# Softmax weights, masked scores and one layer's z kept in PSUM and changed in place, norms on GpSimd, and new instruction orders, in a two-layer graph kernel

## Chip, cores and metric

The kernel runs on one core of a Trainium2 chip. The metric is the time of one launch in microseconds on the device. All 128 graphs are handled by that core in one program.

The core's engines run their own instruction streams and meet through semaphores: TensorE (PE) multiplies into PSUM, eight banks of 512 float32 columns per partition; VectorE (DVE) and ScalarE (ACT) read and write PSUM and SBUF; GpSimd (POOL) works on SBUF; SyncE (SP) issues the DMAs of this kernel.

## What is computed

128 graphs of 128 nodes with 384 features. First a two-layer graph attention (L0), residual and norm, then a 12-head attention (L1), residual and norm:

```python
# L0, for l in 0, 1
u_left  = einsum('bih,bjh->bij', h, h @ W_left[l].T)  / sqrt(384)
u_right = einsum('bih,bjh->bij', h, h @ W_right[l].T) / sqrt(384)
u = u_left * triu(adj) + u_right * swap(triu(adj, 1))
e = exp(u) * adj
ctx = (e / (e.sum(2) + 1e-10)) @ (h @ W_lin[l].T + b_lin[l])
h = relu((ctx - mean) / (std(ddof=1) + 1e-3) * a + b)
x = layernorm(x + h)
# L1
p = softmax(q k^T / sqrt(384) + 2 * adj)   # a row of scores that are all 0 gives 0
x = layernorm(x + (p v) @ Wo.T + bo)
```

## The kernel before

**Tiling.** Graphs go in groups of four (`GROUP`), 32 groups. A pass of the program (`body`, once per engine) handles L0 of one group, L1 of the group before it, and the last pieces of L1 (the `TAIL`: pv, to, po, norm and store of graph 3) of the group before that. There are 34 passes: the first has no L1, the last two no L0. All float32 products are made of three f16 products (hi x hi, hi x lo, lo x hi), so nearly every PSUM result is read twice: ScalarE rounds it to the f16 `_hi` half, VectorE subtracts that from the PSUM value and writes the `_lo` half.

**Stages.** nl(l, 0..5): the left and right products of layer l, 9 matmuls of 512 columns each. hl(l, b): the linear product, 9 of 384. u(l): scores of L0. ctx(l, b): attention times h_lin, whose 385th column is the denominator; `den` takes its reciprocal, ScalarE scales the result (z), `bn` and `z_variance` give mean and variance. Layer 0's z is normed (`norm_z`), transposed on TensorE (th) and put through Relu; layer 1's z goes through `scale_z`, `shift_z`, `resid` (Relu and residual into x1), `y_bn`, `y_variance`, `resid_norm` and `x1_norm`, is split (`x1t`) and turned by two DMA transposes into xT. qk(0..5), v(b): the products of L1. scores(b): 36 small matmuls into the four banks `SC`, 12 heads of 128 columns; VectorE reads them with a custom instruction that adds the bias, negates, and keeps the row's extreme in `nmax`, into `s[b % 2]`. exps: ScalarE's exponents from s. pt: the f16 halves of the exponents. `turn_p`: two DMA transposes of them, pT. pv(b), to(b), po(b): weights times v, transpose, output product. `rs_of` makes 1/sum, set to 0 for an empty row, `live_of` the test for that; `folds` adds s up over the columns on GpSimd in three steps. `po` and `po_stats` on VectorE add the residual and take the last norm's statistics, `y2_power` (GpSimd) the root, `fin` the norm, `store` the DMA out.

**Order and waits.** There is no scheduler at run time: each engine's `body` is a list of calls written out by hand, and each engine runs its list in order. A PSUM bank is used by many stages in turn, in the order of the table `BANK_USES`; before its first matmul into a bank, TensorE waits for the signal in `READ` of the use before. Before the change a bank of scores was free at `s_ok`, VectorE's first read; exps wrote a single SBUF buffer `w`, pt wrote its halves over `s[b % 2]`, so that VectorE's scores(b + 2) waited for the transposes of graph b and for live(b):

```python
dve.wait_ge(live_ok.sem, of.upto(live_ok, n + 1))
dve.wait_ge(pT_in[b % 2].sem, of.upto(pT_in[b % 2], 32 * (n // 2 + 1)))
```

z and x1 were one SBUF buffer each for both layers and for two groups: ctx(0, b) waited for y_ok, and resid for y2_ok.

In the rows, L1322 is any product of `product`, L1332 a transpose, L1386 u, L1446 scores, L1463 pv, L596 ScalarE's copy whatever it copies, L883 and L881 VectorE's lo halves, L923 and L529 pt on VectorE and GpSimd, L948 rs, L1002 nmr of the last norm, L721 fin, L518 folds, L372 the transpose of pT_lo.

## Time and profile before

| | us |
|---|---|
| median of 3 runs | 2750.87 (2749.57 to 2752.33) |
| the profiled execution | 2750.55 |
| its span, first to last instruction | 2748.8 |
| PE, DVE, ACT, POOL busy in the span | 2581.7, 2356.8, 1863.5, 1655.0 |
| granted TensorE clock, mean | 0.986 |

The time of the profiled execution is 1.7 us more than its span. A row of the page or of the grouped view reads: line, engine, operation, output<-inputs, shape, count, busy time and mean ns of one, idle time of the engine before it and what ended most of that. The matmuls of a stream overlap, so the sum of their lengths is more than the time that they take.

### The profile page before, as it was taken

The page shows a single profiled execution, that of the slowest core. Times are in us where ns is not written, and L with a number is a line of the kernel's source. Part 1 is how long each engine was busy: PE and PEld are TensorE (multiplying, and loading weights), DVE is VectorE, ACT ScalarE, POOL GpSimd, SP SyncE. Part 2 cuts the span into 40 slices and gives each one's busy share as a digit, 9 for nine tenths or more (in the row PEclk, how much of TensorE's full clock was granted, in tenths as well). Part 3 has the DMA queues.
Part 4 walks back from the last instruction along what each step waited for, and adds up shares of the span by engine and source line. Part 5 has one row for each costly group of instructions (what it writes and reads, how often), then busy time and mean ns, then how long its engine had stood idle before and what let it go on. Part 6 is the DMA issues. An engine that isn't in the chain of part 4 may idle for free.

```text
span 2748.8 us, 70524 instructions
## 1 busy us (share of the span) xinstructions
PE 2581.7 (94%) x25152; PEld 1527.9 (56%) x25152; DVE 2356.8 (86%) x8074; ACT 1863.5 (68%) x4395; POOL 1655.0 (60%) x1686
## 2 busy tenths in 40 slices
PE   6999999999999999999999999999999999999976
PEld 3555555555555555555555555555555555555543
DVE  4788988889888889888889888889888898888885
ACT  4666776667776667776667776667766677766664
POOL 3556665565666565766565755566655656665644
PEclk9999999999999999999999999999999999999986
DMA  4235343344443343443343443343433433433333
GB/s 157 53 88 104 71 101 86 76 96 82 93 92 92 69 106 73 101 90 85 79 104 70 105 92 74 90 101 73 98 90 77 96 83 92 93 92 71 84 79 67
DMA packets 557742, 242.33 MB, mean 88 GB/s; under 512 B 506704, under 2 KB 539472, under 8 KB 557392
## 3 DMA queue, kind: packets, MB, share of 16 engines
q1 hardware_dynamic: 557392, 237.83, 38.7%
q8 instruction: 200, 3.28, 0.5%
q14 instruction: 150, 1.23, 0.2%
HBM read 86.77 MB, written 25.17 MB: 41 GB/s over the span
## 4 chain that ended last, share of the span: by engine, by line
DVE 41%; PE 38%; issue 10%; ACT 5%; POOL 3%; DMA 2%; SPq 1%; DVEq 0%; ACTq 0%; POOLq 0%
PE psum L1322 36%; DVE nT_lo L883 4%; DVE rs L948 3%; DVE s L912 3%; DVE z L1093 2%; DVE x L1121 2%; DVE y L979 2%; DVE s L923 2%; DVE z L1102 2%; DVE xTin L1157 2%; PE psum L1446 2%; DVE st L987 2%; DVE hl_raw L896 1%; DMA pT_lo<-s 1%; DVE yst L1048 1%
## 5 line engine op out<-in xcount | busy, mean ns | idle before, releaser
L657 ACT ACTIVATE w<-s,nmax 128x128 f32<-128x128 f32 x1536 | 477.6, 391 | 29.6 <-DVE nmax L912 29.4
L1322 PE MATMUL psum<-hT_hi,w_hi 128*128 128x512 f16 x1152 | 439.9, 382 | 34.2 <-DVE nT_lo L883 20.8
L1322 PE MATMUL psum<-hT_lo,w_hi 128*128 128x512 f16 x1152 | 438.3, 380 | 0.0
L1322 PE MATMUL psum<-hT_hi,w_lo 128*128 128x512 f16 x1152 | 437.8, 380 | 0.0
L596 ACT ACTIVATE nT_hi<-psum 128x512 f16<-128x512 f32 x384 | 220.7, 590 | 303.8 <-PE psum L1322 303.8
L912 DVE CUSTOM_DVE_ANT_0 s<-psum,adj 128x128 f32<-128x128 f32 x1536 | 345.6, 284 | 23.0 <-PE psum L1446 19.3
L446 POOL TENSOR_TENSOR hl_lo<-hl_raw,hl_hi 128x384 fp32r<-128x384 f32 x256 | 238.7, 938 | 192.5 <-ACT hl_hi L596 192.5
L518 POOL TENSOR_TENSOR fold<-s 128x768 f32<-128x768 f32 x128 | 243.2, 1900 | 152.6 <-DVE nmax L912 137.2
L883 DVE SCALAR_TENSOR_TENSOR nT_lo<-psum,nT_hi 128x512 f16<-128x512 f32 x384 | 251.8, 683 | 29.5 <-ACT nT_hi L596 29.1
L596 ACT ACTIVATE z<-psum,rden 128x384 f32<-128x384 f32 x256 | 134.2, 575 | 184.5 <-DVE rden L1034 184.5
L529 POOL TENSOR_TENSOR s<-w,s 128x512 f16<-128x512 f32 x128 | 164.1, 1282 | 145.3 <-ACT s L596 145.3
L1322 PE MATMUL psum<-w_hi,hT_hi 128*128 128x384 f16 x768 | 250.5, 326 | 0.0
L1322 PE MATMUL psum<-w_hi,hT_lo 128*128 128x384 f16 x768 | 250.3, 326 | 0.0
L1322 PE MATMUL psum<-w_lo,hT_hi 128*128 128x384 f16 x768 | 250.2, 326 | 0.0
L518 POOL TENSOR_TENSOR fold<-fold 128x384 f32<-128x384 f32 (+1 forms) x256 | 230.8, 901 | 20.1
L596 ACT ACTIVATE s<-w 128x512 f16<-128x512 f32 x384 | 228.8, 620 | 16.9 <-POOL fold L518 13.4
L1322 PE MATMUL psum<-xT_hi,w_hi 128*128 128x512 f16 x576 | 219.8, 382 | 13.2 <-DMA xT_lo<-xTin 13.2
L487 POOL TENSOR_TENSOR yrstd<-yvar,pw 128x4 f32<-128x4 f32 x32 | 32.4, 1013 | 329.8 <-DVE yvar L1068 329.8
L1322 PE MATMUL psum<-xT_lo,w_hi 128*128 128x512 f16 x576 | 219.1, 380 | 0.0
L1322 PE MATMUL psum<-xT_hi,w_lo 128*128 128x512 f16 x576 | 219.1, 380 | 0.0
L1322 PEld LDWEIGHTS psum<-hT_hi,w_hi 128*128 128x128 f16 x1152 | 112.6, 98 | 163.0 <-DVE nT_lo L883 24.4
L923 DVE TENSOR_TENSOR s<-w,s 128x512 f16<-128x512 f32 x256 | 176.7, 691 | 27.7 <-ACT s L596 27.1
(132 smaller groups left out, 7792.3 us busy)
## 6 DMA issues: line engine op xcount, KB each, us to landing
xTin<-xT SPq DMA_DIRECT2D x32, 768.0 KB, 4.4
xres<-x SPq DMA_DIRECT2D x32, 768.0 KB, 5.5
out<-y SPq DMA_DIRECT2D x128, 192.0 KB, 2.0
adjm<-adjM SPq DMA_DIRECT2D x32, 384.0 KB, 5.2
adjT_sb<-adjT SPq DMA_DIRECT2D x32, 256.0 KB, 4.7
adj<-adj SPq DMA_DIRECT2D x32, 256.0 KB, 3.3
x<-weights SPq DMA_DIRECT2D x4, 576.0 KB, 4.6
pT_hi<-s SPq DMA_TRANSPOSE x128, 3.8
```

Source lines behind the costliest of these rows:

```text
L446: nc.gpsimd.tensor_tensor(hl_lo[:, b, 0:FEAT], hl_raw[:, b], hl_hi[:, b, 0:FEAT].bitcast(f32), ALU.subtract).then_inc(hlr_lo[l].sem, 1)
L518: nc.gpsimd.tensor_tensor(fold[:, :, 0:n], src[:, :, 0:n], src[:, :, n:2 * n], ALU.add)\
L529: nc.gpsimd.tensor_tensor(p_lo[b % 2][:, part], w[:].rearrange("p h t -> p (h t)")[:, part], p_hi[b % 2][:, part], ALU.subtract).then_inc( ...
L596: return nc.scalar.activation(dst, src, ACT.Copy, scale=scale)
L657: last = nc.scalar.activation(w[:, m], s[b % 2][:, m], ACT.Exp, bias=nmax[b % 2][:, m:m + 1], scale=-1.0)
L883: nc.vector.scalar_tensor_tensor(dst, src, scale, rounded, ALU.mult, ALU.subtract)\
L912: last = nc.vector.tensor_tensor_reduce(out=s[b % 2][:, m], in0=psum[:, SC[j], c * TOK:(c + 1) * TOK], in1=adj2[:, b], scale=-1.0 / TEMPER ...
L923: nc.vector.tensor_tensor(p_lo[b % 2][:, part], w[:].rearrange("p h t -> p (h t)")[:, part], p_hi[b % 2][:, part], ALU.subtract).then_inc( ...
L948: nc.vector.scalar_tensor_tensor(rs[b % 2][:], live[b % 2][:], 0.0, rs[b % 2][:], ALU.is_gt, ALU.mult) .then_inc(rs_ok.sem, 1)
L979: nc.vector.scalar_tensor_tensor(y2[:, b % 2], bank("po", b)[:, 0:FEAT], 1.0 / WSCALE, x1[:, b], ALU.mult, ALU.add).then_inc(y2_ok.sem, 1)
L987: nc.vector.bn_stats(st2[:], y2[:, b % 2]).then_inc(y2st_ok.sem, 1)
L1322: last = mm(dst, a, b, start=(i == 0), stop=(i == total - 1))
```

## The change

- **Softmax weights in PSUM.** exps write the exponents back into the score bank they came from. pt is now per bank: ScalarE copies 384 columns to the f16 half in a buffer of its own, `p16[b % 2][:, 0]`, and VectorE subtracts it from PSUM into `p16[b % 2][:, 1]` (16 each per pass, none on GpSimd). A score bank is free at `pt_lo`.
- **u in PSUM**: masked and added in place (in two instructions and an addition for two graphs), exp_u reads PSUM. **Relu of th** is written back in place for th's lo half. **Layer 1's z** stays in its ctx bank until the residual has read it; that bank is free at `y_ok`.
- **x1 in two buffers** `xb`: x is loaded by DMA into the one that becomes x1 (`load_res`), the separate `xres` is gone.
- **live_of** only sums; the test for an empty row is two comparisons inside `rs_of`, with intermediates in unused columns of the pv bank; nmax and total get a buffer per graph.
- **Norms as (x - mean) * rstd**: nmr, ynmr and nmr2 are gone. fin and x1_norm move from ScalarE to GpSimd, the additions of 1e-5 from VectorE to GpSimd; the factor of the unbiased deviation moves into inv_std.
- **New orders** on all five engines and a new `BANK_USES`. On TensorE to(3) and po(3) of the tail move from among nl(0, .) to behind u(0), qk(0) ahead of ctx(0, .), hl(1, 0..1) ahead of scores(1), scores(3) behind nl(1, 5), hl(1, 3) stays behind to(1), po(1) and po(2) move among and behind ctx(1, .). On SP load_tri moves behind turn_p(0), store(3) ahead of turn_p(1).

```diff
-        READ = {... "u0": u_read[0], "u1": u_read[1],
-                "c0": z_ok[0], "c1": z_ok[1], "th": th_hi, "qk": qkr_lo, "v": v_sum, "s": s_ok,
+        READ = {... "u0": e_raw[0], "u1": e_raw[1],
+                "c0": z_ok[0], "c1": y_ok, "th": th_lo, "qk": qkr_lo, "v": v_sum, "s": pt_lo,
...
-            uses(("hl0", 0), ("qk", 2), ("s", 0, 4, 8, 12), ("to", 0, 2), ("po", 2)),
+            uses(("nl0", 5), ("u0", 0), ("qk", 2), ("s", 0, 4, 8, 12), ("to", 2), ("c1", 3)),
...
# ScalarE
                 for c in range(KB):
                     m = KB * j + c
-                    last = nc.scalar.activation(w[:, m], s[b % 2][:, m], ACT.Exp, bias=nmax[b % 2][:, m:m + 1],
+                    last = nc.scalar.activation(psum[:, SC[j], c * TOK:(c + 1) * TOK], s[b % 2][:, m], ACT.Exp, bias=nmax[b][:, m:m + 1],
                                                 scale=-1.0)
-            def pt(p, b, r):
-                act.wait_ge(fold1.sem, p.upto(fold1, b + 1))
-                act.wait_ge(p_ok.sem, p.upto(p_ok, TILES * b + r + 2))
-                copy(p_hi[b % 2][:, part], w[:].rearrange("p h t -> p (h t)")[:, part]).then_inc(pt_hi.sem, 1)
+            def pt(p, b, j):
+                act.wait_ge(p_ok.sem, p.upto(p_ok, TILES * b + j + 1))
+                copy(p16[b % 2][:, 0, KB * TOK * j:KB * TOK * (j + 1)], psum[:, SC[j], 0:KB * TOK]).then_inc(pt_hi.sem, 1)
# VectorE
                 if j == 0 and of.l1:
-                    dve.wait_ge(live_ok.sem, of.upto(live_ok, n + 1))
-                    dve.wait_ge(pT_in[b % 2].sem, of.upto(pT_in[b % 2], 32 * (n // 2 + 1)))
+                    dve.wait_ge(fold1.sem, of.upto(fold1, n + 1))
+                if of.l1:
+                    dve.wait_ge(p_ok.sem, of.upto(p_ok, n * TILES + j + 1))
...
+                nc.vector.tensor_tensor(p16[b % 2][:, 1, part], psum[:, SC[j], 0:KB * TOK], p16[b % 2][:, 0, part],
+                                        ALU.subtract).then_inc(pt_lo.sem, 1)
...
-                nc.vector.scalar_tensor_tensor(rs[b % 2][:], live[b % 2][:], 0.0, rs[b % 2][:], ALU.is_gt, ALU.mult)
+                nc.vector.scalar_tensor_tensor(rs[b % 2][:], total[b][:], 0.0, rcp, ALU.is_gt, ALU.mult)\
+                    .then_inc(live_ok.sem, 1)
+                nc.vector.scalar_tensor_tensor(peak, nmax[b][:], 0.0, rcp, ALU.is_lt, ALU.mult)\
+                    .then_inc(live_ok.sem, 1)
+                dve.wait_ge(live_ok.sem, p.upto(live_ok, 2 * b + 2))
+                nc.vector.tensor_tensor(rs[b % 2][:], peak, rs[b % 2][:], ALU.max).then_inc(rs_ok.sem, 1)
...
-                nc.vector.tensor_tensor(uLR[h][:], bank(f"u{l}", h)[:, 0:2 * TRI].rearrange("p (b c) -> p b c", b=2),
-                                        mask[:, 2 * h:2 * h + 2], ALU.mult).then_inc(u_read[l].sem, 1)
+                nc.vector.tensor_tensor(u_right[h][:], dst[:, :, TOK:TRI], mask[:, 2 * h:2 * h + 2, TOK:TRI], ALU.mult)\
+                    .then_inc(u_right_ok[l].sem, 1)
+                nc.vector.tensor_tensor(dst[:, :, 0:TOK], dst[:, :, 0:TOK], mask[:, 2 * h:2 * h + 2, 0:TOK], ALU.mult)\
+                    .then_inc(u_read[l].sem, 1)
...
+                nc.vector.scalar_tensor_tensor(z1(b), z1(b), mv[1][:, b, 0:1], lnrow[:, 0],
+                                               ALU.subtract, ALU.mult).then_inc(za_ok.sem, 1)
...
-                nc.vector.scalar_tensor_tensor(x1[:, b], z[:, b], 0.0, xres[:, b], ALU.max, ALU.add)\
+                nc.vector.scalar_tensor_tensor(xb[1 - p.odd][:, b], z1(b), 0.0, xb[1 - p.odd][:, b], ALU.max, ALU.add)\
# GpSimd
+            def fin(run, b):
+                pool.wait_ge(y2pow_ok.sem, p.upto(y2pow_ok, b + 1))
+                nc.gpsimd.tensor_scalar(y2[:, b % 2], y2[:, b % 2], mv2[:, b % 2, 0:1], rstd2[:, b % 2:b % 2 + 1],
+                                        ALU.subtract, ALU.mult).then_inc(fin_ok.sem, 1)
```

The orders at three places. First VectorE at the seam of two passes, behind the last statistics of ctx(1, .): L1056 / L1039 are the aggregates, L1093 / L1072 scale_z, L1102 / L1081 shift_z, L1121 / L1100 resid, L883 / L873 nl(0, .), L945 and L948 rs_of(3), L960 pv(3). Before:

```order
L1056 BN_AGGR mv1<-st1 128x2 [waits st_ok1] x4
L1058 TENSOR_SCALAR var1<-mv1 128x4 [waits mv_ok1]
L1093 SCALAR_TENSOR_TENSOR z<-z,mv1,lnrow 128x384 x3
L883 SCALAR_TENSOR_TENSOR nT_lo<-psum,nT_hi 128x4x128 [waits nl0_hi] x2
L945 RECIPROCAL rs1<-psum 128x12 [waits pv_full]
L948 SCALAR_TENSOR_TENSOR rs1<-live1,rs1 128x12 [waits live_ok,rcp_ok]
L1075 TENSOR_SCALAR sd_eps1<-sd1 128x4 [waits pow_ok1]
L1077 RECIPROCAL rstd1<-sd_eps1 128x4 [waits eps_ok1]
L960 TENSOR_TENSOR o1<-psum,rs1 128x4x3x32 [waits rs_ok,to_full]
L1093 SCALAR_TENSOR_TENSOR z<-z,mv1,lnrow 128x384
L1102 SCALAR_TENSOR_TENSOR z<-z,rstd1,lnrow 128x384 [waits za_ok,rstd_ok1]
L1102 SCALAR_TENSOR_TENSOR z<-z,rstd1,lnrow 128x384 [waits za_ok]
```

and after the change:

```order
L1039 BN_AGGR mv1<-st1 128x2 [waits st_ok1] x4
L1072 SCALAR_TENSOR_TENSOR psum<-psum,mv1,lnrow 128x384 [waits mv_ok1] x3
L1053 TENSOR_SCALAR sd_eps1<-sd1 128x4 [waits pow_ok1]
L1055 RECIPROCAL rstd1<-sd_eps1 128x4 [waits eps_ok1]
L1072 SCALAR_TENSOR_TENSOR psum<-psum,mv1,lnrow 128x384 [waits mv_ok1]
L1081 SCALAR_TENSOR_TENSOR psum<-psum,rstd1,lnrow 128x384 [waits za_ok,rstd_ok1]
L1081 SCALAR_TENSOR_TENSOR psum<-psum,rstd1,lnrow 128x384 [waits za_ok]
L1100 SCALAR_TENSOR_TENSOR xb0<-psum,xb0 128x384 [waits zb_ok,xres_in]
L1081 SCALAR_TENSOR_TENSOR psum<-psum,rstd1,lnrow 128x384 [waits za_ok]
L873 SCALAR_TENSOR_TENSOR nT_lo<-psum,nT_hi 128x4x128 [waits nl0_hi]
```

The z chain now comes ahead of nl(0, .), and rs_of(3) and pv(3), which wait for TensorE's pv(3), stand behind all of it.

Second VectorE from scores(0, 3) of graph 0 to the first tile of the next graph. After the change (L1089 is th, L1117 v, L913 pt, L924 the sum of live_of, L903 scores):

```order
L1089 TENSOR_TENSOR hT1_lo<-psum,hT1_hi 128x512 [waits th_raw,th_hi]
L1117 SCALAR_TENSOR_TENSOR v_raw<-psum,bias 128x384 [waits v_full,pv_full] x2
L913 TENSOR_TENSOR p16_0<-psum,p16_0 128x384 [waits pt_hi] x4
L1117 SCALAR_TENSOR_TENSOR v_raw<-psum,bias 128x384 [waits v_full,pv_full]
L924 TENSOR_REDUCE total0<-fold 128x12 [waits fold3]
L903 ISA s1,nmax1<-psum,adj2 128x128 [waits s_full,p_ok,fold1]
```

Before, the three v and th were followed at once by the next graph's scores, and graph 0's two pt stood behind three of its four tiles.

Third GpSimd from the last fold of a pass to the last v, where L473 / L475 is weigh, L483 / L485 e_rest, L446 / L448 hl(1, 3), L487 / L489 the powers. Before:

```order
L518 TENSOR_TENSOR fold<-fold 128x12x16 [waits fold2]
L473 TENSOR_TENSOR e<-e,adjT_sb 128x256 [waits e_raw1]
L487 TENSOR_TENSOR rstd<-var,pw 128x1 [waits y2var_ok]
L483 TENSOR_TENSOR e_lo<-e,e_hi 128x256 [waits e_ok1,e_hi_ok1]
L473 TENSOR_TENSOR e<-e,adjT_sb 128x256 [waits e_raw1]
L446 TENSOR_TENSOR hl_lo<-hl_raw,hl_hi 128x384 [waits hl1_hi]
L483 TENSOR_TENSOR e_lo<-e,e_hi 128x256 [waits e_ok1,e_hi_ok1]
L446 TENSOR_TENSOR hl_lo<-hl_raw,hl_hi 128x384 [waits hl1_hi]
L529 TENSOR_TENSOR s<-w,s 128x512 [waits pt_hi,p_ok]
```

and after:

```order
L522 TENSOR_TENSOR fold<-fold 128x12x16 [waits fold2]
L475 TENSOR_TENSOR e<-e,adjT_sb 128x256 [waits e_raw1] x2
L485 TENSOR_TENSOR e_lo<-e,e_hi 128x256 [waits e_ok1,e_hi_ok1] x2
L532 TENSOR_SCALAR var2<-mv2 128x1 [waits y2mv_ok]
L489 TENSOR_TENSOR rstd2<-var2,pw 128x1 [waits y2var_ok]
L541 TENSOR_SCALAR y2<-y2,mv2,rstd2 128x384 [waits y2pow_ok]
L448 TENSOR_TENSOR hl_lo<-hl_raw,hl_hi 128x384 [waits hl1_hi]
```

The subtraction of pt is gone from GpSimd's list, and fin(0) (L541) now stands between the last e_rest and hl_lo(3); three of the four hl_lo moved ahead of the last folds, and so did two biases and the lo halves of x.

## Rows read from the trace of the kernel before

**Rows 1.** The page: span, and busy us (share of the span) xinstructions

```profile
span 2748.8 us, 70524 instructions
...
PE 2581.7 (94%) x25152; PEld 1527.9 (56%) x25152; DVE 2356.8 (86%) x8074; ACT 1863.5 (68%) x4395; POOL 1655.0 (60%) x1686
```

**Rows 2.** The chain that ended last, in order of time: start, us, what

```profile
269.76 13.56 PE psum L1322 x63
...
2599.21 13.56 PE psum L1322 x63
```

**Rows 3.** Windows: stretch, us, busy (x) of each engine, PEclk, DMA share, GB/s

```profile
1185.50:1268.50 83.00, 80.00 (x787) 47.57 (x786) 72.96 (x252) 57.73 (x138) 51.62 (x53) 1.00 0.42 86
```

**Rows 4.** Timeline of TensorE: start, us, operation, [idle before <-releaser]

```profile
1221.72 0.23 PE L1446 MATMUL psum<-qk_hi 32*128 32x128 f16 x4
...
1233.71 0.55 PE L1332 MATMUL psum<-ident,o 128*128 128x128 f32 x3 [0.60 <-DVE o L960]
...
1239.54 0.41 PE L1322 MATMUL psum<-hl_hi,e_hi 128*128 128x386 f32 x1 [0.59 <-DVE y L979]
...
1242.87 0.39 PE L1322 MATMUL psum<-hT_hi,w_hi 128*128 128x512 f16 x1
...
1248.54 0.39 PE L1322 MATMUL psum<-hT_hi,w_hi 128*128 128x512 f16 x1 [0.71 <-DVE nT_lo L883]
```

**Rows 5.** The same timeline, first and last of 36 matmuls of qk

```profile
1191.13 0.39 PE L1322 MATMUL psum<-xT_hi,w_hi 128*128 128x512 f16 x1
...
1198.69 0.38 PE L1322 MATMUL psum<-xT_hi,w_lo 128*128 128x512 f16 x1
```

**Rows 6.** Small instructions: grouped by form; one line's min/median/max ns; the timeline

```profile
L948 DVE SCALAR_TENSOR_TENSOR rs<-live,rs 128x12 f32<-128x12 f32 x128 | 97.2, 760 | 4.6 <-DVE rs L945 0.2
...
L1002 DVE SCALAR_TENSOR_TENSOR nmr<-mv,rstd 128x1 f32<-128x1 f32 x128 | 55.3, 432 | 105.8 <-POOL rstd L487 105.8
...
L945 DVE RECIPROCAL rs<-psum 128x12 f32<-128x12 f32 x128 | 28.6, 223 | 1.0 <-PE psum L1463 0.7
...
L948 DVE SCALAR_TENSOR_TENSOR rs<-live,rs x128: 170/172/1810, 140.1 to 2737.4; 128x12 f32<-128x12 f32 x128
...
1221.58 1.81 DVE L948 SCALAR_TENSOR_TENSOR rs<-live,rs 128x12 f32<-128x12 f32 x1
...
1221.55 1.81 POOL L518 TENSOR_TENSOR fold<-s 128x768 f32<-128x768 f32 x1
```

**Rows 7.** VectorE's groups by form: busy us, mean ns

```profile
L883 DVE SCALAR_TENSOR_TENSOR nT_lo<-psum,nT_hi 128x512 f16<-128x512 f32 x384 | 251.8, 683 | 29.5 <-ACT nT_hi L596 29.1
...
L923 DVE TENSOR_TENSOR s<-w,s 128x512 f16<-128x512 f32 x256 | 176.7, 691 | 27.7 <-ACT s L596 27.1
...
L881 DVE TENSOR_TENSOR oT_lo<-psum,oT_hi 128x384 f16<-128x384 f32 x128 | 71.2, 556 | 11.1 <-ACT oT_hi L596 10.9
```

**Rows 8.** GpSimd's groups by form

```profile
L446 POOL TENSOR_TENSOR hl_lo<-hl_raw,hl_hi 128x384 fp32r<-128x384 f32 x256 | 238.7, 938 | 192.5 <-ACT hl_hi L596 192.5
...
L529 POOL TENSOR_TENSOR s<-w,s 128x512 f16<-128x512 f32 x128 | 164.1, 1282 | 145.3 <-ACT s L596 145.3
...
L502 POOL TENSOR_SCALAR adj<-adj 128x512 f32<-128x512 f32 x32 | 19.8, 619 | 12.8 <-DMA adj<-adj 10.2
```

**Rows 9.** ScalarE's groups by form

```profile
L657 ACT ACTIVATE w<-s,nmax 128x128 f32<-128x128 f32 x1536 | 477.6, 391 | 29.6 <-DVE nmax L912 29.4
...
L596 ACT ACTIVATE s<-w 128x512 f16<-128x512 f32 x384 | 228.8, 620 | 16.9 <-POOL fold L518 13.4
...
L721 ACT ACTIVATE y<-y,nmr,rstd 128x384 f32<-128x384 f32 x128 | 90.1, 704 | 51.6 <-DVE nmr L1002 50.8
...
L596 ACT ACTIVATE oT_hi<-psum 128x384 f16<-128x384 f32 x128 | 62.0, 485 | 42.2 <-PE psum L1332 41.3
```

**Rows 10.** Timeline of SP's DMA queue, the second transpose of graph 3

```profile
1242.74 1.42 SPq L372 DMA_TRANSPOSE pT_lo<-s  x1
```

**Rows 11.** The chain that ended last, in its last 70 us

```profile
2711.78 5.36 DMA pT_lo<-s
```

588 lines of the change are left out of this document (274 added, 314 removed).

## The prediction

> **What bounds the kernel now.** I read the page first: TensorE is busy 94% of the span, VectorE 86%, ScalarE 68%, GpSimd 60% [rows 1]. Then the chain that ended last: its long runs of matmuls come back at the same place of each pass, 28 passes in 2599.21 - 269.76 us, so a pass takes **83.2 us** [rows 2]; there are 30 such passes (pass 2 to pass 31), some 2,496 of the 2,749 us. Then the windows: in one pass TensorE is busy 80.0 of 83.0 us, VectorE 73.0, ScalarE 57.7, GpSimd 51.6 [rows 3]. The busy figure flatters TensorE: 36 matmuls of 512 columns start 0.216 us apart (7.56 / 35), but each is drawn 0.38 us long [rows 5], so after each wait some 0.165 us are counted that a stream would have overlapped. With about 14 waits a pass the work is 80.0 - 2.3 = **77.7 us**, and 5.5 us of a pass are waits. The change does not touch the matmuls, so 5.5 is all it can give, and only by making TensorE's inputs and banks ready sooner.
>
> Where the 5.5 us are: the timeline marks waits for o, y2 and nT_lo, all VectorE's work, in the last third and at the start of a pass [rows 4]; from scores(3) at 1221.7 to nl(0,0) at 1242.9, behind ctx(1,3), it takes 21.2 us [rows 4], of which about 18.4 are matmuls by their spacings, and from there to the matmul behind ctx(0,3) (1191.1 [rows 5], one pass of 83.0 on) it takes 31.3 for 29.3 of work. So some 4.8 us of the 5.5 lie in these two stretches.
>
> **The change part by part (us per pass).**
>
> *VectorE's small instructions.* rs<-live,rs has a median of 172 ns and a mean of 760; nmr, smaller still, a mean of 432. The timeline shows why: one rs took 1.81 us just while GpSimd ran a fold of 1.81 us [rows 6]. The excess over 0.17 is 0.59 x 4 = 2.4 and 0.26 x 4 = 1.0. nmr2 goes for good. That the new instructions of rs_of, which all have a PSUM operand, are not held is my choice: the row nearest to them, the reciprocal from PSUM in the same rs_of, has a mean of 223 ns [rows 6]. So I take all 3.4 as gone; the bound on the other side keeps the 2.4. Also gone: 13 instructions of about 0.15 (variance adds, nmr, ynmr, live), -2.0; new: two more in rs_of per graph, +1.0.
>
> The Trainium skill (SBUF — State Buffer, section "SBUF: two separate sides") says that a VectorE instruction with two SBUF inputs and a GpSimd instruction that reads SBUF exclude each other for a whole instruction, whichever starts first; only its first half is seen here, in the 1.81 beside 1.81. By that rule, GpSimd's stretched instructions shrink as well, since after the change only the four x1_lo subtractions have two SBUF inputs; if instead any small instruction could be held, the 2.4 would stay.
>
> *pt.* Before: 8 subtractions of 512 columns on VectorE (0.69 drawn, 0.61 apart) and 4 on GpSimd (1.28) [rows 8]. After: 16 of 384 columns on VectorE, priced as oT_lo, 0.556 drawn, 0.47 apart [rows 7]: 7.5 against 4.9, **+2.6** on VectorE, -5.1 on GpSimd. ScalarE: 16 copies like oT_hi (0.485) for 12 of 0.620: even [rows 9].
>
> *Operands in PSUM.* Scale, shift, residual, statistics, th and pt now read PSUM and some write it. A 512-column subtraction costs 0.683 with a PSUM input and 0.691 from SBUF [rows 7]: I take reads at no cost, bound +0.07 each. No row shows a VectorE or ScalarE write to PSUM; nearest, ScalarE's exp 0.391 [rows 9]: I take 0, bounds -0.06 to +0.06 per instruction. u is split in two, +0.8 in all.
>
> VectorE's sum: -3.4 - 2.0 + 1.0 + 2.6 + 0.8 = **-1.0**, from 73.0 to about 72.
>
> *Norms to GpSimd.* Six ScalarE instructions of 0.70 go (-4.2) [rows 9]; on GpSimd a tensor_scalar of 512 columns took 0.619, a two-input one of 384 took 0.938 [rows 8]. For 384 columns with one tensor input I take 0.47 (0.619 x 384/512), bound 0.94. Six of them and five small adds of 0.15: +3.6 (bound +6.4), against -5.1 for pt. GpSimd stays near 50.
>
> *What no longer waits.* scores(b+2) no longer waits on VectorE for the transposes of graph b or its live; exps no longer wait for the single w. In return a score bank is free only after exponent, copy and subtraction, not after the first read. So **scores(b+1) on TensorE now waits for pt(b,3)**, and everything behind it queues on TensorE.
>
> **Walking one pass in the new order.** I count from the end of ctx(1,3), with spacings: VectorE 0.47 for 384 columns, 0.60 for 512, 0.53 for scale and shift, 0.63 for three score tiles; exp 0.29; matmul products 1.94 (512), 1.46 (384), pv 0.9, scores 0.6, u 3.05, ctx 0.53.
>
> A, to the end of ctx(0,3), 28.8 of matmuls. VectorE: den, po and bn of the last graphs end at 4.4 (the four aggregates in), scale x3, inv_std, scale, shift x2, residual(0) at 8.8; then residual(1) 10.8 and residual(3) 12.3. z lies in the banks of nl(0,3), nl(0,4), nl(0,5), hl(0,1), and TensorE wants the first at 1.5 + 3.9 + 0.9 + 1.9 = 8.2, then 10.7 and 12.7: 0.6 us lost. x1_lo is done at 19.5; its transpose lands some 4 to 5.4 later (5.36 is one of the longest, [rows 11]), by 25, when qk(0) comes. u ends at 22, e_lo of the first pair is there at 26.5, ctx(0,0) starts at 27.4. I take 1.0 lost in all (before: 2.0).
>
> B, to scores(1), 19.1 of matmuls. th(0) finds z normalised at 35.7 and is due at 37. qk_lo(5) is ready at 41.0, 0.4 after TensorE wants it. Scores 0 on VectorE with th, v and the four pt end at 48.6; TensorE, with v(0..2) and hl(1,0..1) between, comes at 48.6. Lost: 0.5, no margin.
>
> C, to scores(3), 17.1. pt(1,3) ends at 56.8, scores(2) is due at 57.2; pt(2,3) 64.8 against 65.9. v_lo(0) from GpSimd 58.7 against 59.3. Lost: 0.3 to 0.4.
>
> D, to the end of ctx(1,3), 12.7. Here GpSimd is last: from s_ok(0) at 44.4 it runs four folds of 3.6, xt x3, four biases, v x3, hl x3 without a gap and reaches the end of fold(3) at 73.3, then two weigh and two e_rest of 0.7: e_lo(0) 75.5, e_lo(1) 76.2, rstd2 and fin(0), hl_lo(3) 78.3. TensorE is ready for ctx(1,0) at 75.5 and for ctx(1,3) at 78.6; hl(1,3) waits 0.3 for the bank that exp of u holds. Lost: 0.6 (before: 2.9). pt(3) is copied at 77.2, and the two transposes, 1.4 us of queue time each [rows 10] and about 4 from the second one's issue to its landing, are there 1.2 us before pv(3) is due.
>
> Sum: 77.7 + 1.0 + 0.5 + 0.4 + 0.6 = **80.2**; such a walk misses small gaps, so I say **80.3**, 2.9 less than now. 30 x 2.9 = 87.
>
> *Ends.* The first pass has no attention beside it; all products of hl(1,0) now need the whole of th_lo, and hl(0,3), hl(1,3) are the only cover for e: +1.5. In the last 150 us VectorE's z chain no longer stands behind pv(3) (-3) and VectorE's scores no longer wait for a transpose (5.36 us) [rows 11], but each scores waits for pt: -1. Together -2.5 (bounds -8 and +5).
>
> The profiled execution took 2750.6 us (span 2748.8), the median is 2750.9. 2750.6 - 87 - 2.5 = **2661**.
>
> **The rivals.**
>
> *GpSimd sets the end of the pass.* In D it has no slack: if its norm costs 0.94 instead of 0.47 (two of them before hl_lo(3): +0.9) and a fold 0.1 more than the spacing I used (+0.4), ctx(1,3) ends 1.3 to 1.6 later: 81.8, **2706**. For: the 36 us without a gap, and means of folds above their best. Against: GpSimd idles from there to the next pass's s_ok(0) often.
>
> *The score banks.* If exponent, copy and subtraction in a bank take 0.5 us longer than I priced, scores wait four times: 82.2, **2718**. For: no margin in B, and no row for writes to PSUM. Against: ScalarE has 54 of 80 us of work, and its copies with PSUM inputs are cheap.
>
> *Reads from PSUM cost more.* Priced from the bound, 0.07 on the 39 VectorE instructions whose input moves to PSUM is 2.7 us, of which 16 lie in A and some 10 in B and D without cover: +1.8, 82.1, **2715**. The rows speak against (0.683 and 0.691). The Trainium skill (VectorE: DVE Perf Modes, section "The TRN2 errata — SBUF-src ops pay a fixed extra latency per instruction") has 58 cycles fixed from SBUF and 120 from PSUM, which would do just this; the row disagrees and I follow the row.
>
> *Nothing is gained.* The held instructions were covered, and the new order only moves the waits: 83.1, **2747**. Against: the two stretches with 4.9 us of waits both wait for VectorE.
>
> *Slower.* SP's queue holds store(0) ahead of the transposes of graph 3, and store(0) now waits for GpSimd's fin(0), which stands behind fold(3), weigh and e_rest. If GpSimd is late, pT of graph 3 is late, pv(3) near the head of the next pass waits, and all of TensorE behind it. From 1.2 us of lateness it costs one for one, and from 1.2 + 2.9 = 4.1 us the kernel is slower than before. If fold(3) and fin(0) come 5.5 us later than walked: 84.6, **2791**. Against: before, the same queue held store(0), and pT_lo of graph 3, issued at 1242.74 [rows 10], was in time for pv(3), which stands two products of 1.94 behind 1242.87 [rows 4].
>
> **How the numbers follow.** Forecast (79.4 to 81.2 us a pass, 2632 to 2690): 0.62. GpSimd: 0.17. Score banks: 0.06. PSUM reads: 0.04. Nothing gained: 0.05. Slower: 0.06. Range: forecast, GpSimd and most of the two next, **2630 to 2718**. Faster by over 0.2% (5.5 us, about what a measurement of this kernel can tell): 0.89; same 0.05; slower 0.06.
>
> **What would show it.** A pass of 80.3 in the chain's repeats; rs and peak at about 0.17 without a long one; VectorE near 72 and ScalarE near 54 of a pass; exp not above 0.39; GpSimd's tensor_scalar near 0.47; TensorE's waits for o and y2 gone and the largest one at nl(0,3) for the residual. Wrong if TensorE waits for e_lo or hl_lo at ctx(1,.), for pt at scores, or for pT_lo at pv(3).

## The result, and the profile after

The changed kernel took **2730.44 us** (median; 2728.74 to 2731.18), the one before 2750.87. The ratio is 0.992, with a 95% interval of 0.990 to 0.995. So it is faster, by 20 us, where 90 were forecast: 2661 with a range of 2630 to 2718. The direction was right, the size was not, and the time lies outside the range.

The page after; its first lines answer to [rows 1]:

```profile
span 2728.7 us, 69288 instructions
...
PE 2572.6 (94%) x25152; PEld 1521.4 (56%) x25152; DVE 2275.4 (83%) x8170; ACT 1731.8 (63%) x4331; POOL 1792.6 (66%) x1910
...
POOL 41%; PE 32%; ACT 10%; issue 7%; DVE 6%; DMA 3%; SPq 1%; POOLq 0%; ACTq 0%; DVEq 0%
```

VectorE and ScalarE lost 81 and 132 us of busy time. GpSimd gained 138, though it gave up four large subtractions of each pass, and the chain that ended last now runs for 41% of the span through GpSimd, more than through any other engine; before, 3% of it did.

The length of a pass is read from the load of x^T, which SP issues once in each; two of them, 25 passes apart:

```profile
269.46 0.34 SPq L324 DMA_DIRECT2D xTin<-xT  x1
...
2330.63 0.34 SPq L324 DMA_DIRECT2D xTin<-xT  x1
```

(2330.63 - 269.46) / 25 = **82.45 us**; over the 24 passes without the first it is 82.42, and in the kernel before it was 83.19. So a pass gave 0.77 us where 2.9 were forecast: 30 x 0.77 = 23, and what lies outside the 30 passes grew by 3.0 (2748.8 - 30 x 83.19 = 253.1; 2728.7 - 30 x 82.42 = 256.1).

A window of one pass, the same columns as [rows 3]:

```profile
1258.00:1340.30 82.30, 79.41 (x785) 47.10 (x784) 70.31 (x255) 53.23 (x135) 55.35 (x60) 1.00 0.44 88
```

VectorE 70.3 (before 73.0), ScalarE 53.2 (57.7), GpSimd 55.4 (51.6) us. The groups by form (busy us, mean ns of one, idle before) show where the last number comes from:

```profile
L541 POOL TENSOR_SCALAR y<-y,mv,rstd 128x384 f32<-128x384 f32 x128 | 212.3, 1659 | 13.1
L550 POOL TENSOR_SCALAR xb<-xb,ymv,yrstd 128x384 f32<-128x384 f32 x64 | 112.7, 1766 | 3.5
L506 POOL TENSOR_SCALAR adj<-adj 128x512 f32<-128x512 f32 x32 | 19.9, 623 | 11.2 <-DMA adj<-adj 8.4
...
L522 POOL TENSOR_TENSOR fold<-s 128x768 f32<-128x768 f32 x128 | 232.4, 1815 | 364.0 <-DVE nmax L903 364.0
...
L936 DVE SCALAR_TENSOR_TENSOR rs<-total,psum 128x12 f32<-128x12 f32 x128 | 21.3, 167 | 4.4
L938 DVE SCALAR_TENSOR_TENSOR psum<-nmax,psum 128x12 f32<-128x12 f32 x128 | 21.6, 169 | 0.0
```

The norms (L541, L550) take **1.66 and 1.77 us each**, where the prediction had 0.47 with a bound of 0.94, from the row of adj, which is unchanged at 0.62 for 512 columns. The place in the pass does not make a fin long: the shortest of the 128 took 1.647 us, the longest 1.666. The small instructions of rs_of, 0.76 us before [rows 6], are down to 0.17, as forecast.

What the norms do to TensorE is seen at two places of each pass. First GpSimd and TensorE at the end of the pass (timeline: start, us, operation, [idle before <-releaser]):

```profile
1309.43 1.44 POOL L485 TENSOR_TENSOR e_lo<-e,e_hi 128x256 fp32r<-128x256 f32 x2
1310.84 0.23 POOL L532 TENSOR_SCALAR var<-mv 128x1 f32<-128x1 f32 x1
1311.15 0.58 POOL L489 TENSOR_TENSOR rstd<-var,pw 128x1 f32<-128x1 f32 x1
1311.84 1.67 POOL L541 TENSOR_SCALAR y<-y,mv,rstd 128x384 f32<-128x384 f32 x1
1313.47 0.87 POOL L448 TENSOR_TENSOR hl_lo<-hl_raw,hl_hi 128x384 fp32r<-128x384 f32 x1
```
```profile
1314.39 0.45 PE L1297 MATMUL psum<-hl_hi,e_hi 128*128 128x386 f32 x1 [0.82 <-POOL hl_lo L448]
```

fin(0) stands in front of hl_lo(3), and ctx(1,3) waits 0.82 us for that. Then, 25 us sooner, fin(3) in front of fold(1), whose sum VectorE awaits (total(1), 0.90 idle) with pt(1,3) queued behind it; pt(1,3) frees the score bank:

```profile
1285.51 1.66 POOL L541 TENSOR_SCALAR y<-y,mv,rstd 128x384 f32<-128x384 f32 x1
1287.13 1.81 POOL L522 TENSOR_TENSOR fold<-s 128x768 f32<-128x768 f32 x1
1289.03 1.67 POOL L522 TENSOR_TENSOR fold<-fold 128x384 f32<-128x384 f32 x2
...
1290.73 0.35 DVE L924 TENSOR_REDUCE total<-fold 128x12 f32<-128x192 f32 x1 [0.90 <-POOL fold L522]
1291.00 0.55 DVE L913 TENSOR_TENSOR p<-psum,p 128x384 f16<-128x384 f32 x1
...
1291.60 0.23 PE L1421 MATMUL psum<-qk_hi 32*128 32x128 f16 x4 [0.82 <-DVE p L913]
```

The wait names VectorE's p here; what set it is the fold on GpSimd that total(1), in front of that pt, had to wait for. Over the whole run (TensorE's waits: us in total, times, longest):

```profile
PE psum L1421 <- DVE p L913: 34.8, 32, 7.4
PE psum L1297 <- POOL hl_lo L448: 24.7, 31, 0.8
...
PE psum L1297 <- DVE xb L1100: 15.2, 30, 1.2
```

### The profile page after: what moved, and what is told of

It reads as the page before. It is cut to its first block, busy times and chain, and to the rows that moved or that the text cites. A ratio compares the mean times of both kernels' runs of the same rounds, so it can differ in the third digit from the quotient of the medians.

```text
span 2728.7 us, 69288 instructions
## 1 busy us (share of the span) xinstructions
PE 2572.6 (94%) x25152; PEld 1521.4 (56%) x25152; DVE 2275.4 (83%) x8170; ACT 1731.8 (63%) x4331; POOL 1792.6 (66%) x1910
## 4 chain that ended last, share of the span: by engine, by line
POOL 41%; PE 32%; ACT 10%; issue 7%; DVE 6%; DMA 3%; SPq 1%; POOLq 0%; ACTq 0%; DVEq 0%
PE psum L1297 28%; POOL fold L522 12%; POOL hl_lo L448 4%; POOL xb L465 4%; POOL y L541 4%; ACT psum L667 4%; POOL hT_lo L440 4%; POOL v_lo L456 3%; POOL rstd L489 3%; DMA xT_lo<-xTin 2%; PE psum L1361 2%; POOL mask L432 2%; POOL xb L550 2%; ACT p L612 2%; ACT hT_hi L712 2%
## 5 line engine op out<-in xcount | busy, mean ns | idle before, releaser
L667 ACT ACTIVATE psum<-s,nmax 128x128 f32<-128x128 f32 x1536 | 469.7, 363 | 75.8 <-DVE nmax L903 75.8
L522 POOL TENSOR_TENSOR fold<-s 128x768 f32<-128x768 f32 x128 | 232.4, 1815 | 364.0 <-DVE nmax L903 364.0
L1297 PE MATMUL psum<-hT_hi,w_hi 128*128 128x512 f16 x1152 | 438.2, 380 | 27.4 <-DVE xb L1100 15.2
L903 DVE CUSTOM_DVE_ANT_0 s<-psum,adj 128x128 f32<-128x128 f32 x1536 | 338.8, 286 | 28.7 <-PE psum L1421 28.5
L448 POOL TENSOR_TENSOR hl_lo<-hl_raw,hl_hi 128x384 fp32r<-128x384 f32 x256 | 237.0, 937 | 129.9 <-ACT hl_hi L612 129.7
L913 DVE TENSOR_TENSOR p<-psum,p 128x384 f16<-128x384 f32 x512 | 261.6, 547 | 23.9 <-ACT p L612 23.2
L873 DVE SCALAR_TENSOR_TENSOR nT_lo<-psum,nT_hi 128x512 f16<-128x512 f32 x384 | 247.9, 678 | 21.4 <-ACT nT_hi L612 21.4
L612 ACT ACTIVATE p<-psum 128x384 f16<-128x384 f32 x512 | 222.6, 481 | 1.8
L541 POOL TENSOR_SCALAR y<-y,mv,rstd 128x384 f32<-128x384 f32 x128 | 212.3, 1659 | 13.1
L522 POOL TENSOR_TENSOR fold<-fold 128x384 f32<-128x384 f32 (+1 forms) x256 | 204.0, 797 | 20.1
L612 ACT ACTIVATE qk_hi<-psum 128x512 f16<-128x512 f32 x192 | 114.7, 597 | 157.1 <-PE psum L1297 153.2
L1361 PE MATMUL psum<-nT_hi,hT_hi 128*64 128x192 f16 x1536 | 191.7, 248 | 1.4 <-DVE nT_lo L873 1.4
```

Of the source, the lines that this page charges most:

```text
L448: nc.gpsimd.tensor_tensor(hl_lo[:, b, 0:FEAT], hl_raw[:, b], hl_hi[:, b, 0:FEAT].bitcast(f32), ALU.subtract).then_inc(hlr_lo[l].sem, 1)
L522: nc.gpsimd.tensor_tensor(fold[:, :, 0:n], src[:, :, 0:n], src[:, :, n:2 * n], ALU.add)\
L541: nc.gpsimd.tensor_scalar(y2[:, b % 2], y2[:, b % 2], mv2[:, b % 2, 0:1], rstd2[:, b % 2:b % 2 + 1], ALU.subtract, ALU.mult).then_inc(fin_ ...
L612: return nc.scalar.activation(dst, src, ACT.Copy, scale=scale)
L667: last = nc.scalar.activation(psum[:, SC[j], c * TOK:(c + 1) * TOK], s[b % 2][:, m], ACT.Exp, bias=nmax[b][:, m:m + 1], scale=-1.0)
L873: nc.vector.scalar_tensor_tensor(dst, src, scale, rounded, ALU.mult, ALU.subtract)\
```

## The experiments

Times are medians; the kernel before took 2750.0 to 2752.1 beside them, and the difference to 2730.4 is taken straight, so differences of a few us between kernels say little. Ratios are against the kernel before of the same set of runs. The edits are shown shortened: buffer numbers and waits are left out. The three price lists ran once each, the others four or five times.

Three explanations were set against each other: (A) the length of GpSimd's norms, (B) score banks that come free too late whatever GpSimd does, (C) many small gaps that the walk had missed.

**fin_act.** `fin` on ScalarE, its bias formed on GpSimd.

```
-   nc.gpsimd.tensor_scalar(y2[b], y2[b], mean, rstd2, ALU.subtract, ALU.mult)
+   nc.gpsimd.tensor_scalar(nmr2, mean, rstd2, -1.0, ALU.mult, ALU.mult)
+   nc.scalar.activation(y2[b], y2[b], ACT.Identity, bias=nmr2, scale=rstd2)
```

> The last norm fin goes back to ScalarE (Identity with scale and bias); GpSimd instead forms its bias, one column, behind each power. All else as in the changed kernel. Theory A (GpSimd's norms of 1.66 us make the pass long: fin(3) in front of fold(1), fin(0) in front of hl_lo(3), fin(1) in front of z_power): TensorE's waits of 0.8 us at scores(2), 0.8 at ctx(1,3) and part of the 0.5 at nl(0,3) go, 1.3 to 1.8 us of a pass, 2675 to 2692 us against 2730. Theory B (the score bank is free too late because exponent, copy and subtraction stand on it, whatever GpSimd does): the wait for p at scores(2) stays above 0.6, the pass loses at most 0.5, 2715 or more. Theory C (the walk missed many small gaps): GpSimd gets shorter by 6 us of a pass and the time hardly moves, 2725 or more.

2727.9 (ratio 0.991, 0.990 to 0.993). The waits at scores(2) and ctx(1,3) shrank as A said (hl_lo: 24.7 to 0.2 us in all; p: 34.8 to 11.4), which rules B out as the cause of them. The time by itself does not: it lies in the ranges of B and C and not in that of A. Nearly all was given back, since TensorE now waited for pT_lo, 68.8 us in 59 pieces where the changed kernel waits 7.6:

```profile
PE psum L1443 <- DMA pT_lo<-p: 68.8, 59, 5.1
...
PE psum L1426 <- DVE p L918: 11.4, 3, 7.4
```

**x1n_act** and **norms_act.** The two norms of x1 on ScalarE, alone and with fin_act.

> Only the two norms of x1 go back to ScalarE, ahead of x1's four copies; GpSimd forms their bias columns. fin stays on GpSimd. Theory A: the copies of x1 end some 0.5 us sooner, the wait for xT_lo at qk(0) (0.4 us) goes, nothing else: 0.2 to 0.4 us of a pass, 2718 to 2725. Theories B and C: no change, 2728 to 2732. If ScalarE's two norms of 0.7 delay x1's copies instead: 2730 to 2740.

2724.1 (0.990, 0.989 to 0.992), as A said; the gain on 2730.4 is only 6 us.

> Both edits together: no norm is left on GpSimd. Theory A: the parts add up, 1.6 to 2.1 us of a pass, 2667 to 2682, near the 2661 that was forecast with norms of 0.47. Theory B: 2712 or more. Theory C: 2722 or more.

2717.5 (0.988, 0.986 to 0.989): far from A's number, and by its time alone in B's range (2712 or more). But the wait for p is at 11.4 us here too, as in fin_act, and what TensorE waits for is pT_lo, 66.8 us in 57 pieces. The trace shows SP's queue and the product that waits:

```profile
1312.48 0.35 SPq L307 DMA_DIRECT2D out<-y  x1
1312.93 1.31 SPq L373 DMA_TRANSPOSE pT_hi<-p  x1
1314.29 1.95 SPq L375 DMA_TRANSPOSE pT_lo<-p  x1
```
```profile
1318.63 0.18 PE L1452 MATMUL psum<-v_hi,pT_hi 128*128 128x33 f16 x1 [0.70 <-DMA pT_lo<-p]
```

pt_hi of graph 3 was written at 1310.5, but its transpose stands behind store(0), which waits for fin(0), done at 1312.46. That is the place of the prediction's slower rival.

**norms_act2.** store(0) behind the transposes of graph 3, y2_power(3) ahead of folds(0), fin(3) behind qk(4).

```
     turn_p(p, 2)
-    store(p, 0)
     turn_p(p, 3)
+    store(p, 0)
     store(p, 1)
```

> The kernel norms_act (2717.5 us, where TensorE waits 0.7 us at pv(3) and 0.3 at pv(2) for pT_lo) with three moves: store(0) behind the transposes of graph 3 in SP's queue, y2_power(3) ahead of folds(0) on GpSimd, fin(3) behind qk(4) on ScalarE, so that store(3) no longer holds the transposes of graph 1. If the gain of the norms' move was given back in SP's queue (theory A with the named rival of the prediction in place of it): both waits for pT_lo go, 1.0 us of a pass, about 2687; pass 80.4. If they only uncover the next wait (o, oT_lo or p): at least 2705.

**2780.1** (1.011, 1.010 to 1.013), slower than before. The move was mine and it broke something else: y2 has two buffers, po(2) on VectorE writes the one that store(0) reads, and all of VectorE queues behind it:

```profile
1337.96 0.56 DVE L986 SCALAR_TENSOR_TENSOR y<-psum,xb 128x384 f32<-128x384 f32 x1 [2.51 <-DMA out<-y]
```

TensorE then waits 2.42 us for the residual, and its granted clock falls behind that wait: 0.80, 0.50 and 0.84 in the 6 us from 1344, so for some us to the lower of its two levels, 1.2 GHz. Of 25 passes in the middle 16 have such a stretch; they took 84.3 us on average and the other nine 83.8, against 80.2 in norms_act3 below, so the clock is the small part of the loss. pool_order has it in 22 of 25 passes.

**norms_act3.** The same with three buffers of y2 (graphs 0 to 3 use 0, 1, 2, 1).

> norms_act2 (2780 us, where VectorE waits 2.51 us at po(2) for store(0), which the move behind the transposes of graph 3 made late) with three buffers of y2 for two, so that po(2) need not wait for store(0). All norms on ScalarE. If store(0)'s place is what gave the gain back in norms_act, and the shared y2 what lost it in norms_act2: the wait of VectorE for out<-y goes, no pT_lo wait at pv(3) or pv(2), 2670 to 2690 us. If neither: 2715 or more.

**2660.1** (0.967, 0.965 to 0.968), 10 us below the range that I gave. With no norm on GpSimd and the queue out of the way, the kernel runs where the forecast was. C falls with this: small gaps are not what kept the changed kernel 69 us from the forecast.

**pool_order**, **pool_order3** and **order_clean.** The norms stay on GpSimd at 1.66 us, at better places: y2_power(3) and fin(3) ahead of folds(0), fin(0) behind hl_lo(3), store(0) behind the transposes. pool_order has two y2 buffers and the mask behind z_power(1), pool_order3 three buffers, order_clean three buffers and the mask where it was.

> The changed kernel with its norms left on GpSimd at 1.66 us, and only its places changed: y2_power(3) and fin(3) ahead of folds(0), where GpSimd idles for 11 us; fin(0) behind hl_lo(3); the mask behind z_power(1), where GpSimd idles for 8 us; store(0) behind the transposes of graph 3. If it is the place of the norm that costs (what stands behind it): waits at scores(2), ctx(1,3) and part of nl(0,3) go, 1.3 to 1.8 us of a pass, 2677 to 2692 us. If it is GpSimd's load as such or VectorE's instructions stretched beside it: 2715 or more.

2816.4 (1.024, 1.023 to 1.026): the same wait for store(0) as in norms_act2 spoiled it.

> pool_order (2816 us: norms of 1.66 at better places on GpSimd, where VectorE waited at po(2) for store(0)) with three buffers of y2. If place decides (the norms cost by what stands behind them): 2665 to 2690. If their length decides wherever they stand: 2715 or more.

2721.4 (0.989, 0.988 to 0.991), and not clean either: the moved mask held a four-column VectorE instruction on the path to the residual.

```profile
1317.14 1.81 POOL L433 TENSOR_TENSOR mask<-adjm,keep 128x768 f32<-128x768 f32 x1
...
1317.21 1.76 DVE L1053 TENSOR_SCALAR sd_eps<-sd 128x4 f32<-128x4 f32 x1 [0.57 <-POOL sd L490]
```

> The changed kernel with subtract and multiply norms of 1.66 us on GpSimd, three y2 buffers, store(0) behind the transposes of graph 3, y2_power(3) and fin(3) ahead of folds(0), fin(0) behind hl_lo(3); the mask stays where it was. pool_order3 (2721) less the 1.6 us a pass that the mask cost there. If place decides: 2665 to 2685, as good as short norms. If length decides: 2715 or more. In between: both.

2702.9 (0.983, 0.981 to 0.984), in between: place alone (with the third buffer and the moved store) brings 27 of the 75 us by which the fastest kernel below beats the changed one, the rest needs shorter norms. The wait for hl_lo at ctx(1,3) is gone, but the one for the residual (xb) at nl(0,3) rose from 15.2 to 46.2 us in all: two norms now stand in front of z_power(1).

**The price lists** fin_forms, fin_forms2, fin_forms3: the changed kernel with its fins, and in the last two x1's norms, at the same places in other forms, most of which leave out a part of the norm.

> A price list, with wrong values: fin(0) on GpSimd as tensor_scalar with two constants, fin(1) with one per-partition column and one constant, fin(2) with one column alone, fin(3) as a tensor_tensor with the mean's column spread over 384 columns; the norms of x1 keep two columns. If each column operand costs: 0.47 for fin(0) (0.623 x 384/512), about 1.06 for fin(1) and fin(2), 0.94 to 1.0 for fin(3), 1.77 for x1. If it is the place or VectorE beside it that makes them 1.66, all four stay near 1.66. The time is 2700 to 2725 by theory A, since about 2.4 us of GpSimd's fins go.

> The second price list, with wrong values: fin(0) as two multiplications by constants, fin(1) by a column and a constant, fin(2) a column times and a column plus, fin(3) a constant times and a constant plus, x1's norms as one multiplication by a column and as a tensor_tensor with that column spread. If the first list's 1.5 came of subtract as first operation: 0.47, about 0.6, about 0.7, 0.5 in turn. If only two equal operations with constants run at 0.47 (the adj row) and every other tensor_scalar is slow: 0.47, then 1.2 to 1.7 for the rest, and 0.83 for the spread one.

> The third price list, wrong values: fin(0) plus a column, times a column; fin(1) times a column, minus a column; fin(2) times a column alone; fin(3) minus and times columns on half of the columns (192); x1's first norm times a column plus a column, its second plus a constant, times a constant. If what is slow is an addition ahead of the multiplication: 1.66 for fin(0), 0.66 for fin(1), x1 0.66 and about 1.6. If single operations are slow too (1.25 and 1.46 in the two lists): fin(2) 1.2 to 1.4. fin(3) gives the slope: 0.83 and a bit if it goes by the column.

The groups that decide, in the order fin_forms (three lines), fin_forms2 (three), fin_forms3 (three), a fence each:

```profile
L543 POOL TENSOR_SCALAR y<-y 128x384 f32<-128x384 f32 x32 | 48.6, 1519 | 2.8
...
L547 POOL TENSOR_SCALAR y<-y,mv 128x384 f32<-128x384 f32 x32 | 39.9, 1247 | 3.0
...
L549 POOL TENSOR_TENSOR y<-y,mv 128x384 f32<-128x384 f32 x32 | 26.4, 826 | 2.5
```
```profile
L547 POOL TENSOR_SCALAR y<-y,rstd,mv 128x384 f32<-128x384 f32 x32 | 21.1, 660 | 3.4
...
L545 POOL TENSOR_SCALAR y<-y,rstd 128x384 f32<-128x384 f32 x32 | 19.0, 594 | 3.3
L543 POOL TENSOR_SCALAR y<-y 128x384 f32<-128x384 f32 x32 | 16.6, 519 | 2.8
```
```profile
L546 POOL TENSOR_SCALAR y<-y,rstd,mv 128x384 f32<-128x384 f32 x32 | 53.5, 1672 | 3.5
...
L550 POOL TENSOR_SCALAR y<-y,mv,rstd 128x192 f32<-128x192 f32 x32 | 32.8, 1024 | 3.5
...
L544 POOL TENSOR_SCALAR y<-y,mv,rstd 128x384 f32<-128x384 f32 x32 | 21.3, 665 | 3.5
```

| fin on GpSimd, 384 columns, fp32 in SBUF | ns |
|---|---|
| x const, x const | 519 |
| x const, + const | 515 |
| x column, x const | 594 |
| x column, + column | 660 |
| + column, x column | 665 |
| - const, x const | 1519 |
| - column, x const | 1588 |
| - column, x column (the changed kernel) | 1659 |
| x column, - column | 1672 |
| one operation alone: - column, x column | 1247, 1258 |
| - column, x column, 192 columns | 1024 |
| tensor_tensor, minus a spread column | 826 |

Neither the column operands (about 0.07 each) nor an addition ahead of the multiplication is what costs, against what I expected of the third list. A tensor_scalar of two operations that holds a **subtract**, in either slot, takes 1.0 us more than the same with add, and one with a single operation is slow too (1.46 at x1 in fin_forms2). The row of adj, which I had priced the norm by, is two multiplications. The lists took 2701.2, 2636.2 and 2674.7 us. fin_forms2 differs from the changed kernel only in the form of its six norms: 94 us for that alone.

**norm_madd** and **fin_madd.** The norm in the fast form: times rstd, plus (-mean x rstd), everything on GpSimd at its old place; fin_madd leaves x1's norms slow.

```
-   tensor_scalar(y2[b], y2[b], mean, rstd2, ALU.subtract, ALU.mult)
+   tensor_scalar(nmr2, mean, rstd2, -1.0, ALU.mult, ALU.mult)
+   tensor_scalar(y2[b], y2[b], rstd2, nmr2, ALU.mult, ALU.add)
```

> The changed kernel with all six norms still on GpSimd, in the same places, but as times rstd plus (-mean x rstd), with the bias column formed by one more tensor_scalar of one column each, in place of minus mean, times rstd. If the price of the form is the loss (two columns with multiply and add took 0.66 in the price list, subtract and multiply 1.66 in the changed kernel): a norm and its column cost 0.66 + 0.35, 0.65 less than before at each fin, 2.3 for 3.5 at x1. The waits at scores(2), ctx(1,3) and nl(0,3) go; the price list ran at 2636 with 0.35 us less at each fin, so 2636 to 2655 us. If what the price list gained came of something else than the norms' length: 2700 or more.

2675.3 (0.972, 0.971 to 0.974).

> The same for the four fins alone; the two norms of x1 stay subtract and multiply (3.5 us for both). The difference to norm_madd is the price of x1's norms on the way to qk(0). If the fins carry most: 2645 to 2665. If x1's norms carry half or more: 2680 to 2700.

2690.3 (0.978, 0.976 to 0.979). So of the 55 us of norm_madd the fins carry 40 and x1's norms 15. (The time of fin_madd alone lies in the range that I gave to the other case; both kernels came out higher than I expected.) The 2675 stand 20 above the range that I gave; I put that down to the bias columns: 0.26 us each on GpSimd at fin and 0.47 at x1, on the same path.

**norm_addm**, **norm_addm3**, **norm_addm_act.** Plus (-mean), times rstd; -mean is made by VectorE, or, in norm_addm_act, by ScalarE.

```
+   nc.scalar.activation(nm2, mean, ACT.Copy, scale=-1.0)      (norm_addm_act)
-   nc.gpsimd.tensor_scalar(y2[b], y2[b], mean, rstd2, ALU.subtract, ALU.mult)
+   nc.gpsimd.tensor_scalar(y2[b], y2[b], nm2, rstd2, ALU.add, ALU.mult)
```

> The changed kernel with its six norms on GpSimd in the same places, as plus (-mean), times rstd (0.67 in the third price list); VectorE forms -mean, one small instruction behind each bn_aggr and one behind y_variance. Against norm_madd (2675) GpSimd saves 0.35 us at each fin and 0.96 at x1. If the walk of the prediction is right once the norms are cheap (it had 0.47): 2655 to 2665. If it was too slow elsewhere, as the cheap fins of the second price list (2636) say: 2630 to 2645. If VectorE's added small instructions cost more than GpSimd saves: 2675 or more.

2664.5 (0.968, 0.967 to 0.970), 3 us above the forecast of 2661.

> norm_addm with the moves of norms_act3: three y2 buffers, store(0) behind the transposes of graph 3, y2_power(3) and fin(3) ahead of folds(0). If places still matter at 0.67 a norm: 5 to 15 us less than norm_addm. If cheap norms have made their places free: within 4 us of it.

2663.0 (0.968, 0.966 to 0.969): with short norms their places are free.

> norm_addm with -mean formed by ScalarE (copies of one or two columns with scale -1, where ScalarE idles) instead of VectorE; all else, orders and GpSimd's 0.67 us norms too, as in norm_addm. If VectorE's five small instructions stood on the path (0.8 us of a pass, the residual's wait at nl(0,3) is what differs from the price list): 2636 to 2645 us, and the waits for xb at nl(0,3) shrink. If they were covered: 2660 to 2668, and the price list's 2636 came of its wrong values or its shorter norms.

**2655.4 (0.965, 0.964 to 0.967), the fastest kernel that computes the whole norm**, 95 us under the kernel before and 75 under the changed kernel. It lies between the two expectations: the wait for the residual shrank as said (the weight loads behind nl(0,3): norm_addm, then norm_addm_act),

```profile
PEld psum L1305 <- DVE xb L1108: 36.7, 62, 1.5
```
```profile
PEld psum L1317 <- DVE xb L1120: 16.4, 55, 1.8
```

but 0.3 us a pass came back at ctx(1,3), since fin(0) waits for its -mean in ScalarE's queue (21.3 us in all for the four fins).

**rs_sbuf.** The reciprocal and peak of rs_of back in SBUF, in the changed kernel.

```
-   rcp, peak = (bank("pv", b)[:, c:c + HEADS] for c in (400, 416))
+   rcp, peak = sb("rcp", [HEADS]), sb("peak", [HEADS])
```

> The changed kernel with the reciprocal and the peak of rs_of back in SBUF, so that its three small VectorE instructions again have two operands in SBUF. If the held instructions came of two SBUF operands beside GpSimd: their means rise from 0.17 to 0.4 to 0.8 us with single ones of 1.8, VectorE's busy time by 3 to 6 us of a pass is possible, the time to 2745 or more. If it was the old order or the 13 small instructions instead: means stay at 0.17 and the time within 3 us of 2730.

**2842.8** (1.034, 1.032 to 1.035), 112 us more than the changed kernel. The three instructions (groups by form), and one of them beside a fold of GpSimd's:

```profile
L936 DVE SCALAR_TENSOR_TENSOR rs<-total,rcp 128x12 f32<-128x12 f32 x128 | 72.8, 569 | 4.4
...
L938 DVE SCALAR_TENSOR_TENSOR peak<-nmax,rcp 128x12 f32<-128x12 f32 x128 | 69.5, 543 | 0.0
L941 DVE TENSOR_TENSOR rs<-peak,rs 128x12 f32<-128x12 f32 x128 | 66.1, 517 | 4.4
```
```profile
1347.16 1.84 DVE L938 SCALAR_TENSOR_TENSOR peak<-nmax,rcp 128x12 f32<-128x12 f32 x1
...
1347.17 1.80 POOL L523 TENSOR_TENSOR fold<-s 128x768 f32<-128x768 f32 x1
```

The excess is (569 + 543 + 517 - 507) ns x 4 = 4.5 us a pass on VectorE. A pass took 85.8 us (25 in the middle) for 82.4, so 3.3 of it came through, the rest of the 112 us lies outside these passes. The granted clock dips here too, in 12 of the 25, but those took 85.8 us like the other 13: the clock is not what cost.

**before_rs.** One small part of the change alone, in the old kernel.

```
-   nc.vector.reciprocal(rs[b % 2][:], src[:, :, HEAD])
+   rcp = bank("pv", b)[:, 400:400 + HEADS]
+   nc.vector.reciprocal(rcp, src[:, :, HEAD])
...
-   scalar_tensor_tensor(rs, live, 0.0, rs,  ALU.is_gt, ALU.mult)
+   scalar_tensor_tensor(rs, live, 0.0, rcp, ALU.is_gt, ALU.mult)
```

> The kernel before with one edit: the reciprocal of rs_of goes to 12 spare columns of its own PSUM bank, so that rs<-live,rs has one operand in SBUF instead of two. If two SBUF operands are what is held: its mean falls from 760 to about 170 ns, VectorE's busy time by 2.4 us of a pass. If those 2.4 stood on the path (the prediction has them in stretch D and at o): 2720 to 2735. If they were covered: 2748 or more.

**2709.9** (0.984, 0.983 to 0.986), 42 us less than before, 20 less than with the whole change, and 10 below the range that I gave. The instruction of [rows 6] now reads:

```profile
L949 DVE SCALAR_TENSOR_TENSOR rs<-live,psum 128x12 f32<-128x12 f32 x128 | 21.4, 167 | 4.7 <-DVE psum L946 0.4
```

All 128 of them lie between 166 and 169 ns. 0.59 us x 4 = 2.4 us of VectorE's time went and the pass fell from 83.19 to 81.78, by 1.4.

## Why the prediction missed

**The step that failed: the price of a norm on GpSimd.** It was scaled from a row of the same operation name (0.619 x 384 / 512 = 0.47), with 0.94 as bound from a two-input instruction. It measured 1.66 and 1.77. The bound was the nearest other row and was no bound: no row of the kernel before shows that one tensor input costs less than two. All six norms together took 10.2 us of a pass for the 2.8 of the forecast, and GpSimd's pass 55.4 for 50. In norm_addm_act, with norms of 0.66 and 0.80, it is 49.9; without the norms that is 45.7 there and 45.2 in the changed kernel, where the sum had 47.3, so the rest of that term was 2 us too high. What the norms' form cost the kernel is read from fin_forms2: 2730.4 - 2636.2 = 94 us, more than the 69 that were missed.

```profile
1239.00:1319.06 80.06, 79.50 (x787) 47.58 (x786) 70.67 (x256) 54.06 (x141) 49.92 (x59) 1.00 0.47 92
```

The line is a pass of norm_addm_act, in the columns of [rows 3].

**The mechanism was named, as a rival, and under-priced.** "GpSimd sets the end of the pass" had 81.8 us and 2706 with a norm of 0.94, at a chance of 0.17. With the 1.66 that was measured in its sum, 2 x 1.19 on top of 80.3, it gives 82.7; a pass took 82.4. That the two agree is luck: the rival puts both norms into stretch D, and D lost 0.5 of the 2.4. It saw fin(0) ahead of hl_lo(3), and stretch D's slack of nothing; it did not follow fin(3) through fold(1), total(1) and pt(1,3) to the score bank, where as much was lost. That chain goes from GpSimd to VectorE to TensorE and is only seen by asking what is queued behind each waiting instruction.

**The sum was otherwise close, its terms less so.** With the norms short or gone, three different kernels run at 2664.5, 2660.1 and 2655.4, against 2661. In norm_addm_act a pass takes 80.06 us (25 passes), forecast 80.3. But fin_forms2 comes nearest to what the forecast assumed (norms of 0.52 to 0.66 at the fins, nothing else changed), and it ran at 2636 with a pass of 79.4: the walk was about 0.9 us a pass too slow, 25 us in all, and with norms of 0.47 the kernel would have been below 2661. The two parts of its sum were both off, against each other. It had 77.7 us of matmuls and 2.5 of waits; in the pass of fin_forms2 from 1192.5 to 1272.0 the profile marks no wait of TensorE at all, and it lasts 79.5 us, so TensorE's own time is nearer to 79.4 than to 77.7. Stretch by stretch, between the same points of TensorE's timeline, changed kernel and norm_addm_act: nl(0,0) to the end of ctx(0,3) 29.2 and 27.8; to scores(1) 19.3 and 19.3 (walk: 19.6); scores(1) to scores(3) 18.1 and 17.4 (walk: 17.5); scores(3) to nl(0,0) 16.1 and 15.7. Between these two kernels B lost nothing, C lost 0.7 through fin(3) and D 0.5; A lost 1.4, in waits for the residual at nl(0,3), where fin(1) stands ahead of z_power(1), and for xT_lo at qk(0), where x1's norms stand ahead. The walk cuts A and D elsewhere, at the end of ctx(1,3); there norm_addm_act has 29.1 for the 29.8 walked and 14.3 for 13.3, so B and C were right and A and D off by 0.7 and 1.0, against each other.

**Point by point.** VectorE near 72: 70.3. ScalarE near 54: 53.2. exp not above 0.39: 0.363 into PSUM, for 0.391 into SBUF. rs and peak at 0.17, without a long one: yes, the longest took 0.171. The reads from PSUM at no cost: the residual took 0.544 us (from SBUF before 0.548), scale 0.606 (0.611), shift 0.616 (0.611), and pt 0.547 for its 384 columns; that rival falls. The higher fixed cost from PSUM that the Trainium skill gives (VectorE: DVE Perf Modes, section "The TRN2 errata — SBUF-src ops pay a fixed extra latency per instruction") does not show in these durations. The waits for o and y2 gone from the pass: yes. The largest at nl(0,3): no, at scores(2) and ctx(1,3). GpSimd's tensor_scalar near 0.47: no. One sum of a rival is off by 2 us: 83.1 a pass is 2745 by the others' sum, not 2747, which decides nothing.

**The held instructions were worth what was said, and on the path.** The forecast took 3.4 us of VectorE's time a pass for them. before_rs shows that 2.4 of it alone give 1.4 us of the pass, rs_sbuf that the new order, with three such instructions a graph, loses 3.3 a pass without the PSUM operands. In the old order this one part gives 42 us; what the rest of the change gives by itself was not tried apart. The large fold's own mean fell too, from 1.90 us to 1.82 in the changed kernel, but not in before_rs (1.90), so rs was not what stretched it. Instructions with one SBUF input can be held as well: sd_eps, four columns, took 1.76 us beside the mask (1.81) in pool_order3, where its mean is 0.94, and never more than 0.171 in the changed kernel. The prediction counted only the four x1_lo subtractions as still exposed, and that was too few. The Trainium skill (SBUF — State Buffer, section "Who interferes with whom") has a clause for this that the prediction left out: tensor_scalar can also contend with GpSimd, in modes that take both SBUF ports. The 1.76 beside 1.81 agrees with it.

**Ends.** -2.5 forecast, +3.0 measured, 5.5 us of the 69 that were missed. In the last pass, without layer 0 beside it, TensorE waits 7.4 us for pt at scores and 15.2 for o; the wait for pt was named and its length was not. It wasn't tried apart.

**The slower rival's place is real.** store(0) ahead of graph 3's transposes did not bite in the changed kernel, since the pass was late anyway; once the norms were out of the way it took back some of the gain at pv(3), with 0.70 us in the pass shown (norms_act), where TensorE waits 66.8 us for pT_lo in the whole run and 4.6 in norms_act3. Moving it needs a third y2 buffer (norms_act2 against norms_act3: 120 us).

**What stays open.** fin_forms2, one run, is at 2636, 19 us under the best kernel that computes the whole norm; 9 of it are the wait for hl_lo at ctx(1,3) behind -mean (31 x 0.3 us), for the rest I have only that its fins were shorter by up to 0.15 us. And why a subtract is slow in tensor_scalar and not in tensor_tensor (hl_lo, a subtraction, takes 0.94 for two inputs) no run here tells.

## What to carry to other kernels

An instruction moved to an engine is priced by a row of its exact form: the operations and the kind of their operands too, not the name and the shape alone; where the trace has none, the bound is open upwards and one cheap run of several forms is worth more than any scaling. A tuned, gapless stretch on a helper engine (here 36 us of GpSimd) multiplies each such error by the places that stand behind it, across engines. And a large change is worth taking apart: one operand moved to PSUM, alone, gave 42 us where all of the change gave 20.

## What the hardware showed that I had not expected

- On GpSimd a tensor_scalar of 384 fp32 columns takes 0.52 us with two constants, 0.66 with two columns, add and multiply in either order, 1.0 more as soon as one of the two is a subtract (1.52 and 1.66), and 1.25 with one operation alone. For - and x it is 1.02 at 192 columns; from the two sizes I estimate 3.3 ns a column and some 0.39 us fixed. VectorE shows no such price: its norm of x1 took 0.476 in the form minus and times (x1n_act) and 0.471 as times and plus (before).
- A 12-column VectorE instruction with two SBUF operands can run as long as the GpSimd instruction beside it (1.84 beside 1.80, with a median of 0.164). With one operand in PSUM it takes 0.17 (512 of them in before_rs and the changed kernel). A tensor_scalar with one SBUF operand was held the same way (1.76 beside 1.81).
- VectorE's own norm of x1 took 0.61 us while GpSimd ran x1's other two, in the form minus and times (the changed kernel) as in plus and times (norm_addm, norm_addm_act), and 0.48 where those stood on ScalarE (x1n_act) or behind two small instructions (norm_madd). GpSimd's norm of x1 took 0.80 beside it and 0.67 in norm_madd.
- After TensorE had waited 2.42 us in norms_act2 its granted clock went to 0.80, 0.50 and 0.84 in the next 6 us and was back at 1.00 from 1350 on. In the changed kernel and in norm_addm_act no pass between the 5th and the 29th load of x^T was granted less than 1.00.
